# Expert choice of the first two batches inside the scan, and six of their eight tiles sent there by GpSimd

## What is computed

```python
def _L1_ffn_ref(hidden_states, gate_w, w_gate, w_up, w_down):    # E = 32, K = 8, 2048 rows
    probs = jax.nn.softmax(x @ gate_w, axis=-1)
    w, sel = jax.lax.top_k(probs, K)
    w = w / jnp.sum(w, axis=-1, keepdims=True)
    ...
    pos = jnp.arange(P) - start[se]          # rank of a row among those of its expert
    slot = jnp.where(pos < C, se * C + pos, E * C)
    ...
    g = jnp.einsum('ech,ehi->eci', xg, w_gate)
    u = jnp.einsum('ech,ehi->eci', xg, w_up)
    y = jnp.einsum('eci,eih->ech', jax.nn.silu(g) * u, w_down).reshape(E * C, H)
    out = jnp.zeros((T + 1, H), x.dtype).at[t_slot].add(w_slot[:, None] * y)
...
x = x + _L1_xattn_ref(ctx_1024, _layernorm(x, axis=-1), ...)     # the scan
x = x + _L1_ffn_ref(_layernorm(x, axis=-1), ...)                 # the experts
```

## Time and profile before

| | |
|---|---|
| median of 3 runs | 1883.29 us (1882.07 to 1884.48) |
| the profiled execution | 1881.68 us, span 1879.5 us |
| TensorE | 1554.0 us busy, 83% of the span |
| VectorE | 1308.7 us, 70% |
| ScalarE | 911.0 us, 48% |
| GpSimd | 791.8 us, 42% |
| sends of rows (L1474) | 128, 129.1 us busy, mean 1009 ns |
| mean granted clock of TensorE | 0.897 of full speed |

### The profile page before, as it was taken

The page is one execution under the profiler, slowest core; times in us unless marked ns, Lnnn a source line. Parts: engine busy times, 40 slices in busy tenths (PEclk is TensorE's granted clock), DMA queues, the critical chain, the costliest instruction groups (busy, mean ns, idle before and its releaser), DMA issues. The chain is left out here.

```text
span 1879.5 us, 26432 instructions
## 1 busy us (share of the span) xinstructions
PE 1554.0 (83%) x9418; PEld 1319.2 (70%) x9426; DVE 1308.7 (70%) x1901; ACT 911.0 (48%) x1577; POOL 791.8 (42%) x481
## 2 busy tenths in 40 slices
PE   5857778677528987996898799975899999999896
PEld 3444355454428976895897689855789999999785
DVE  6677586786659989999998999642445555555452
ACT  3444545445234444344444534432466666666463
POOL 1010000010045456445655643177735766762555
PEclk9878888888758997997999799987999999999998
DMA  7988799984682492375359236379998999999876
GB/s 213 343 281 275 274 321 368 333 270 157 210 314 95 175 357 74 119 283 222 106 188 370 82 118 218 145 266 338 382 365 232 250 269 253 256 260 223 226 170 85
DMA packets 187942, 445.48 MB, mean 237 GB/s; under 512 B 41616, under 2 KB 43664, under 8 KB 177568
## 3 DMA queue, kind: packets, MB, share of 16 engines
q1 hardware_dynamic: 115040, 283.37, 44.7%
q0 software_dynamic: 31760, 74.48, 16.8%
q10 hardware_dynamic: 41008, 85.89, 12.6%
HBM read 246.77 MB, written 205.28 MB: 241 GB/s over the span
## 5 line engine op out<-in xcount | busy, mean ns | idle before, releaser
L1441 POOL TENSOR_TENSOR mix_st<-mix_Bb,mix_du 128x2048 f32<-128x2048 f32 x64 | 293.3, 4583 | 268.2 <-DVE mix_st L2225 255.7
L2217 DVE TENSOR_TENSOR_SCAN mix_st<-mix_YY,mix_st 128x512 f32<-128x512 f32 x256 | 312.0, 1219 | 46.0 <-POOL mix_st L1441 24.0
L1895 ACT ACTIVATE mix_YY<-mix_dt,mix_A 128x512 f32<-128x512 f32 x256 | 176.9, 691 | 276.5 <-DVE mix_st L2217 272.3
L1492 POOL DMA_INDIRECT out_x<-moe_ys,moe_meta x130 | 210.5, 1619 | 190.1 <-ACT moe_ys L2032 84.6
L1611 PE MATMUL mix_G<-mix_xThi,mix_wup 128*128 128x256 f32 x1408 | 273.0, 291 | 14.5 <-issue 13.6
L1611 PEld LDWEIGHTS mix_G<-mix_xThi,mix_wup 128*128 128x128 f32 x1408 | 231.8, 199 | 17.6 <-issue 16.2
L1793 PE MATMUL mix_Dp<-moe_xhi,moe_whi 128*128 128x288 f32 x768 | 234.5, 305 | 2.0 <-ACT moe_xhi L1995 1.5
L1793 PE MATMUL mix_Dp<-moe_xhi,moe_wlo 128*128 128x288 f32 x768 | 228.9, 298 | 0.0
L1793 PE MATMUL mix_Dp<-moe_xlo,moe_whi 128*128 128x288 f32 x768 | 228.7, 298 | 0.0
L2357 DVE TENSOR_TENSOR moe_xlo<-mix_G,moe_xhi 128x512 fp32r<-128x512 f32 (+1 forms) x160 | 102.2, 638 | 170.5 <-ACT moe_xhi L1995 167.9
L1637 PE MATMUL mix_YY<-mix_ident,mix_st 128*128 128x128 f32 x1024 | 145.1, 296 | 86.2 <-DVE mix_st L2225 86.2
(11 more groups left out here) (237 smaller groups left out, 3064.9 us busy)
## 6 DMA issues: line engine op xcount, KB each, us to landing
x_by_expert<-front_zeros ACTq DMA_DIRECT2D x16, 4480.0 KB, 24.1
mix_wup<-w_halves SPq DMA_DIRECT2D x44, 1024.0 KB, 5.5
moe_raw<-in_ew SPq DMA_DIRECT2D x32, 1280.0 KB, 8.5
moe_xt<-x_by_expert SPq DMA_DIRECT2D x128, 256.0 KB, 8.6
mix_wdn<-w_halves SPq DMA_DIRECT2D x44, 512.0 KB, 6.4
front_idx<-in_idx SPq DMA_DIRECT2D x44, 384.0 KB, 9.0
w_halves<-front_wst SPq DMA_DIRECT2D x44, 384.0 KB, 7.9
mix_Bb<-bc_rows SPq DMA_DIRECT2D x16, 1024.0 KB, 9.4
```

The source lines that it names most:

```text
L1441: nc.gpsimd.tensor_tensor(st[:, g % STBUF, :, :], Bb[:, q, :, :], du[:, k % 2, :].unsqueeze(1).to_broadcast([P, NG, S]), ALU.mult).then_in ...
L1492: pool.indirect_dma_start(out=out_rows, out_offset=bass.IndirectOffsetOnAxis(ap=meta[0:rows, e % MBUF, j, 0:1].bitcast(U32), axis=0), in_= ...
L1895: nc.scalar.activation(dA, dt[:, k % 2, :], ACT.Exp, scale=A[:, c, m:m + 1]).then_inc(da_ready, 1)
L2217: nc.vector.tensor_tensor_scan(r, dA, r, 0.0, ALU.mult, ALU.add).then_inc(scanned, 1)
```

## The change

Batches 0 and 1 (`EARLY` = 2) are chosen in the slots of batches 2 and 3: their transposes at place 15 of the batch before and place 0, from `x2`; shift, exponent and the eight largest at place 1, ranks at place 2, places at place 3, weights at place 4. Their scratch lies in the half of `y` that is free then, and their logits and ranks in a bank of `T`, in which up products are formed from place 4 on. The stored rows get 560 columns; SP stores the columns of numbers and weights (`store_meta`) at place 5 and loads three tiles of a batch back (`load_waiting`) into a spent buffer, `xn` for tiles 0 to 2 and `y[:, 1]` for tiles 3 to 5. POOL sends from there in places 8 to 16, three sends in most slots (`SENDS_AT`), 24 per buffer. Tiles 6 and 7 (`ON_CHIP` = 2) are loaded into `XB` at the end of the scan and sent after it with batches 2 and 3, k outermost as before. POOL's constants are made at slot 6. The choice after the scan is that of batches 2 and 3 alone, with filler between them.

```diff
+EARLY = NB - 2
+STAGED = 3
+ON_CHIP = EARLY * TT - 2 * STAGED
+SENDS_AT = ({8: 3, 9: 2, 10: 3, 11: 3, 12: 3, 13: 3, 14: 3, 15: 3, 16: 1}, {9: 2, 10: 3, 11: 3, 12: 3, 13: 3, 14: 3, 15: 3, 16: 4})
...
+        waiting = [Place(nc, "mix_", at, at + 8192)(f"waiting{w}", [P, STAGED, PITCH], F32)
+                   for w, at in enumerate((row_at, small_at))]
...
-            bank = YY[:, b, :] if b < 2 else Dp[:, b - 2, :]
+            bank = T[:, 1, :] if b < EARLY else YY[:, b - EARLY, :]
...
+            def store_meta(b):
+                sp.wait_ge(meta_ready, b + 1)
+                sp.wait_ge(ids_made, 2 * b + 2)
+                sp.dma_start(s["XN"][b][:, D:PITCH].rearrange("(t p) n -> p t n", p=P), meta_of(b)).then_inc(meta_out, 16)
+
+            def load_waiting(w):
+                if w == 0:
+                    sp.wait_ge(zT_ready, TT * EARLY)
+                else:
+                    sp.wait_ge(x3_ready, NB - 1)
+                sp.wait_ge(xn_out, 16 * w + 16)
+                sp.wait_ge(meta_out, 16 * w + 16)
+                sp.dma_start(waiting[w][:, :, :], xn_rows[w * STAGED * P:(w + 1) * STAGED * P, :].rearrange(
+                    "(t p) n -> p t n", p=P)).then_inc(waiting_in, 16)
...
+                if l == 5 and b >= NB - EARLY:
+                    store_meta(b - 2)
+                if l == 7 + b - EARLY and b >= NB - EARLY:
+                    load_waiting(b - EARLY)
...
+            def early_ids(b):
+                pool.wait_ge(x3_ready, b + 1)
+                nc.gpsimd.iota(meta_of(b)[:, :, 0:1].bitcast(I32), pattern=[[P, TT], [1, 1]], base=b * S,
...
+            def send_waiting(w, first, end):
+                if first == 0:
+                    pool.wait_ge(filled, 16 * (FILLS + 2))
+                    pool.wait_ge(waiting_in, 16 * w + 16)
+                    pool.wait_ge(where_ready, w + 1)
+                for j in range(first, end):
+                    k, n = divmod(j, STAGED)
+                    send(w * STAGED + n, k, waiting[w][:, n, :])
+
+            def sends_on_chip(k):
+                if k == 0:
+                    pool.wait_ge(xb_in[0], 16)
+                for i in range(2 * STAGED, EARLY * TT):
+                    send(i, k, XB[:, i, :])
...
+                if l == 12 and 0 < b <= EARLY:
+                    early_ids(b - 1)
+                w, at = (b - EARLY, l) if l > 1 else (b - 1 - EARLY, l + UNITS)
+                if w >= 0 and at in SENDS_AT[w]:
+                    done = sum(n for slot, n in SENDS_AT[w].items() if slot < at)
+                    send_waiting(w, done, done + SENDS_AT[w][at])
...
+            done = sum(n for slot, n in SENDS_AT[1].items() if slot < UNITS)
+            send_waiting(1, done, STAGED * TOP)
             last_scale(2, 0)
+            sends_on_chip(0)
             last_scale(2, 1)
-            pool.wait_ge(ids_made, 2)
-            pool.wait_ge(filled, 16 * (FILLS + 2))
-            for k in range(TOP):
+            pool.wait_ge(ids_made, 2 * EARLY + 2)
+            sends(EARLY, 0)
+            sends(EARLY + 1, 0)
+            for k in range(1, TOP):
                 if k > 1:
                     pool.wait_ge(e_xT_ready, NT * (k - 2) + 2)
-                for b in range(NB):
-                    sends(b, k)
+                sends_on_chip(k)
+                sends(EARLY, k)
+                sends(EARLY + 1, k)
...
+                if h == 0 and b >= NB - EARLY:
+                    pe.wait_ge(rT_copied, TT * (b - 1))
+                if h == 1 and b >= NB - EARLY:
+                    pe.wait_ge(rank_read, b - 1)
...
+            def early_transposes(b, t):
+                n = TT * b + t
+                if t == 0:
+                    pe.wait_ge(norm_ready[2], TT * b + TT)
+                    pe.wait_ge(h_ready, HALVES * (b + 2) - 1)
+                else:
+                    pe.wait_ge(rT_copied, n)
+                for c in range(DC):
+                    last = nc.tensor.transpose(T[:, 0, c * P:(c + 1) * P], x2[:, t, c * P:(c + 1) * P], ident[:, :])
+                last.then_inc(rT_ready, 1)
...
+            def logits(b, t):
+                if b + t == 0:
+                    pe.wait_ge(g_in, 16)
+                if b < EARLY and t == 0:
+                    pe.wait_ge(h_ready, HALVES * (b + 2))
+                if b == EARLY and t == 0:
+                    pe.wait_ge(scanned, NG * ALL)
+                if b == EARLY + 1 and t == 0:
+                    pe.wait_ge(y_copied, NB * DC)
+                pe.wait_ge(rT_copied, TT * b + t + 1)
+                for c in range(DC):
+                    last = nc.tensor.matmul(choice_bank(b, 0, t, t + 1), columns(b, t)[:, c, :], gw[:, c, :],
+                                            start=(c == 0), stop=(c == DC - 1))
+                last.then_inc(logits_ready, 1)
+
...
+                if l == 0 and EARLY <= b < NB:
+                    early_transposes(b - 2, 2)
+                    logits(b - 2, 0)
+                    logits(b - 2, 1)
...
+                    if b >= EARLY:
+                        ranks(b - 2)
...
+                if l == UNITS - 1 and 0 < b <= EARLY:
+                    early_transposes(b - 1, 0)
+                if l == 0 and EARLY <= b < NB:
+                    early_transposes(b - 2, 3)
+                    logits(b - 2, 2)
...
+                if l == UNITS - 1 and 0 < b <= EARLY:
+                    early_transposes(b - 1, 1)
+                if l == 0 and EARLY <= b < NB:
+                    logits(b - 2, 3)
...
+            transposes_and_logits(EARLY)
             for t in range(TT):
                 last_z_transposes(t)
-            transposes_and_logits(1)
-            ranks(0)
-            transposes_and_logits(2)
-            transposes_and_logits(3)
+            ranks(EARLY)
+            pe.wait_ge(rT_copied, TT * (EARLY + 1))
+            stay_busy(20, T[:, 1, :])
+            transposes_and_logits(EARLY + 1)
-            for b in range(1, NB):
-                stay_busy(10)
-                ranks(b)
-            pe.wait_ge(rank_read, 1)
+            stay_busy(10, Dp[:, TT - 1, :])
+            ranks(EARLY + 1)
...
+                    if c == 0:
+                        act.wait_ge(logits_ready, TT * (b - 1))
+                    if c == 2:
+                        act.wait_ge(meta_out, 16 * (b - 1))
+                    if c == 3:
+                        act.wait_ge(where_ready, b - 1)
...
+                    if b == NB - 1 and t == 0:
+                        for k in range(TOP):
+                            act.wait_ge(sent[k], 16 * STAGED)
...
+                if b < EARLY and t > 1:
+                    act.wait_ge(logits_ready, n - 1)
+                stage = T[:, t % 2 if b >= EARLY else 0, :]
...
+                    if l == UNITS - 1 and 0 < b <= EARLY and t == 3:
+                        rows_to_columns(b - 1, 0)
+                    if l == 0 and b >= EARLY and t != 1:
+                        rows_to_columns(b - 2, max(1, t))
+                    if l == 1 and b >= EARLY and t == 1:
+                        exponent(b - 2)
...
+                        dve.wait_ge(rT_ready, TT * b)
...
+                if l == 1 and b >= EARLY:
+                    shift(b - 2)
...
+                if l == 1 and b >= EARLY:
+                    choose_top(b - 2)
+                if l == 3 and b >= EARLY:
+                    place_key(b - 2)
+                if l == 4 and b >= EARLY:
+                    row_weights(b - 2)
...
+                if l == 1 and b >= EARLY:
+                    choose_mask(b - 2)
+                if l == 3 and b >= EARLY:
+                    place_rows(b - 2)
...
+            shift(EARLY)
+            choose(EARLY)
+            row_weights(EARLY)
+            place(EARLY)
+            shift(EARLY + 1)
+            choose(EARLY + 1)
+            place(EARLY + 1)
+            row_weights(EARLY + 1)
```

276 lines of the change are left out of this document (144 added, 132 removed).

## The result

| | before | changed |
|---|---|---|
| median of 4 runs, us | 1882.88 | 1853.09 (1850.97 to 1854.28) |
| profiled execution, us | 1881.68 | 1852.71 |
| its span, us | 1879.5 | 1850.9 |
| first transposes of the first expert | 1242.09 | 1242.44 |
| first tile of the ninth expert | 1414.44 | 1383.48 |

The changed kernel takes 0.984 of the time before, interval 0.982 to 0.986: **29.8 us faster**. The median is 7 us above the forecast of 1846 and inside the range. (The prediction's "six experts later" is the ninth expert's first tile.

A forecast was written before the change was run, and what follows sets the result against it. PE and DVE bound the scan's second halves, PE the late experts; between them POOL's sends make PE wait. 1881.7 - 13.3 - 39.2 + 14.2 + 1.5 = 1844.9 us profiled, 1846 as a median, range 1830 to 1867.

The forecast's parts named there:

- The first expert earlier: After the scan: only batches 2 and 3 left to choose, fewer sends before the first expert; 13.3 us gained, bounds 9 to 15.
- Experts at PE's pace: Experts 1 to 6: 10 sends per round take 12.8 us, under PE's 17.59; 39.2 us gained in all.
- The 2 us of shorter waits and the 2.5 us of clock: First expert: shorter tile waits gain 2 us; less PE idling beforehand, so a faster clock, gains 2.5 (0 to 5).
- the allowance for DMA waits: Early experts: 4 us of waits left (bounds 0 and 12), as transfers need about 17.4 us of PE's 17.59.
- the DMA rival: Early experts: DMA sets their pace, periods 19.5 us instead of 17.59, 11.5 and 6 us lost, 1864; chance 0.13.
- The scan, +15.7: Batches 2 and 3 of the scan: costs of 14.2 us, plus 1.5 for waits and sends.
- (a): End of slot 15: ACT copies the first transposed tile before the next slot's first decay; 2.6 us a batch.
- (b): Slots 1, 3 and 4, where DVE is full: its choice, places, weights and shift cost 3.8 us a batch.
- (c): Slot 4: the new weight product stands ahead of DVE's product of states, beside POOL's work; 0.7 us a batch (0 to 1.7).
- The waits and sends: Scan: ACT's wait for all first sends 0.5 us (0 to 4), the sends themselves 1 us in all.
- POOL behind in the scan: Rival: sends over 1.51 us push POOL's product over DVE's; 7 slots per batch lose 1.8 us each, 1871; chance 0.12.
- The other rivals: Up weights starved (1898, chance 0.03), handshakes over 20 us a batch (0.02), early sends unfinished in the scan (1860, 0.04).

The follow-up runs named there:

- e10: Changed kernel with POOL's rounds of sends for experts 1, 2 and 3 cut in two by waits, at most five sends under way; 1871.83 us.
- e1: Changed kernel without PE's 20 filler products between batch 2's ranks and batch 3's transposes; last statistics to first transposes 28.58 us, 3.1 more than the changed kernel.
- e2: Changed kernel with the split of the first expert's weights moved earlier on ACT and DVE; end of logits to first transposes 16.29 us in place of 18.09.
- e4: Changed kernel with ACT's copy of the first transposed tile behind the next slot's first decay, not ahead; scan stretch 445.20 us in place of 448.22.
- e11: Changed kernel with the edits of e2 and e4 and a later gate for the send rounds of experts 3 to 7; 1852.45 us, 0.986 of the kernel before.
- e12: Changed kernel with the edits of e2 and e4 and the third expert's weights loaded behind its third tile; 1848.74 us, 0.983 of the kernel before.
- e6: Changed kernel without the 48 sends of tiles 0 to 5 in the scan; scan stretch 447.99 us, against 448.09 in e5.
- e9: The kernel before, unchanged, run again with its profile; scan stretch 436.08 us, against 436.07 in its first trace.
- e5: The changed kernel, unchanged, on a chip where the kernel before takes 1947.0 us; 1884.17 us, 0.968 of the kernel before.
- e3: Changed kernel with 68 filler products instead of 48 ahead of the first expert's tiles; first transposes 28.36 us after the statistics in place of 25.5.

## Why the prediction came out as it did

The gains were forecast 11.4 us too large and the costs in the scan 3.5 us too dear; these errors cancel in part, and the rest is the 7.8 us by which the profiled execution lies above 1844.9. The mechanisms were right in the main.

**What bounded the kernel.** Right. POOL's rounds of 16 sends were the pace of the first experts; with 10 a round the period is PE's 17.59 us from the fourth expert on. e10 shows the same from the other side: 25.1 us of waits put into three rounds make the stretch 18.4 us longer.

**The first expert earlier, -13.3: the mechanism right, the size 3.5 us too large.** Two steps were mis-sized, by 2.0 and 1.8 (the rest of the path came out 0.3 shorter). The logits of batch 3 end 7.4 us after the statistics (1216.95 to 1224.35), not 5.4: I had batch 3's transposes free at once, and PE was still at its middle filler, which is 1.4 of the 2.0. e1 shows that this is no plain loss, since without it the clock falls and the logits end 9.1 us after the statistics; leaving out that filler doesn't bring my 5.4. And the first send of batch 3 took 2.81 us where I had 1.27 with its gap: DVE's split of the first expert's weights, which I had put down as ending "at about 1221", started only at 1229.74, in the same microsecond. I had priced just this collision in the scan, from the earlier trace rows, and not here. e2 took it away and got back 1.80. The Trainium skill, SBUF — State Buffer, section "SBUF: two separate sides", has the lock held for the whole instruction; the trace agrees that the send waits to an instruction's end, 2.81 us against 0.97, and DVE's three operations of 0.98 weren't delayed. The trace goes further in one thing: the send doesn't get in between two operations that follow each other. In another it differs: the same section has it that DVE's `tensor_tensor` didn't stall a DMA, and here this very operation did; the measurement decides.

**Experts at PE's pace, -39.2: 7.9 us too large.** The wait of 13.28 us is gone in full. The 2 us of shorter waits and the 2.5 us of clock inside the first expert are almost not there: from the first transposes to the third expert's first tile it takes 27.49 us, against 28.11 before without that wait, 0.6 us of 4.5. The clock is still 0.53 there, and PE had idled for 4.14 us ahead of it, from the end of the filler at 1238.3, where I had "about a microsecond"; the long send is 1.8 of them. The other 4 us are the allowance for DMA waits, 4 of them forecast and 8.0 found (113.55 us for six periods of 17.59), 7.1 of them in the first period. That was inside my bounds of 0 and 12, but not my value. Only 4.8 of the 8.0 are waits for tiles (4.32 in the first period, 0.23 and 0.28 later). The other 2.8 of the first period hold no wait; they lie behind that of 4.32, where PE's granted clock is 0.57 (1276 to 1284). So this wait cost its own length and the slow microseconds after it, and my sum had no term for that. The reason that I had weighed, 17.4 us of transfers against 17.59, was right as a mean, and wrong for the first period: there the rounds of sends for two later experts, 1280 KB of weights and five tiles meet (share 1.02). So the DMA rival held in part, at the third expert only, and at 4.8 us of waits with 2.8 of clock behind them, of its 17.5.

**The scan, +15.7: 3.5 us too dear.** The slots of the last batch, from one of POOL's products of inputs to its next, in us:

| slot | 0 | 1 | 2 | 3 | 4 |
|---|---|---|---|---|---|
| before | 11.05 | 8.68 | 13.51 | 8.78 | 9.68 |
| changed | 13.45 | 10.18 | 13.21 | 9.81 | 10.94 |
| e4 | 11.97 | 10.17 | 13.22 | 9.82 | 10.92 |

(a) The late decay was seen where it was forecast, 2.62 us of DVE's idle time, and slot 0 is 2.4 us longer (2.3 in batch 2) where I had 2.6. The cause that I gave is 1.5 to 1.6 a batch of it (e4, e11 and e12), and 0.9 stays when the copy is moved. (b) and (c) were too dear: slots 1 to 4 are 3.5 us longer (3.6 in batch 2) where I had 4.5 (3.8 and 0.7); no run separates the two. That is 1.9 of the 3.5 us. The waits and sends, put at 1.5 us, cost 0.1 (e6), which is 1.4 more.

**POOL behind in the scan.** Its condition, a send over 1.51 us, was met: in slot 11 of the last batch a slot's three sends take 9.48 - 4.62 = 4.86 us, 1.62 each, the first of them 1.80 behind DVE's product. The collision that it feared came too, once a batch: in slot 10 DVE's product of states took 2.93 us, 1.7 more than in e6, because POOL's product was 2 us late (I had 1.2). So the price of 1.8 us was right for one slot and not for seven: in slots 11 and 12 DVE's product takes 1.55 us and then 1.20. And even in that slot it cost no time, since the scan is the same to 0.1 us without the sends. The step that failed is the way from a lag of DVE to the time, with the count of slots; the threshold and the collision were right. POOL's last product of the batch comes 1.1 us late, and the long slots at the end take that in.

**The other rivals.** Up weights landed in 7.0 us between 1120 and 1160, not 5.5, far from 12.8. The early sends ended in the scan as the diff says.

**What I can't account for.** -1.85 us ahead of the changed part and +2.36 behind the ninth expert. Both are what two executions differ by. The mark at 748.47 and 746.62 is at 746.62 in e9 too, which is the kernel before, and between 746.4 and 749.9 in all twelve runs. The last stretch was 465.06 and 464.8 in the kernel before, 466.0, 464.7 and 464.5 in e5, e11 and e12, and from 461.6 (e3) to 468.9 (e4) in the rest, e6 aside. Why two of the chips take 60 and 64 us longer for the kernel before, and one of them 31 for the changed one, isn't settled: e5 places it, in two parts, and the run that was to test the cause (e10) came to a chip that doesn't show it.

## What to carry to other kernels

When sends or loads are taken off a path, price the first period after it by what meets there, not by the mean: here the mean had slack, and the first period kept 7 of the 8 us lost, nearly 3 of them by the slower clock behind a wait. When you move a step, list what will run beside it at its new time; a collision that was priced in one place was missed in another, and cost 1.8 us. A collision of two engines has a price on the engine and another on the time: here 1.7 us of the one were 0 of the other. And before removing filler work that seems to be in the way, measure what the clock behind it is worth.

## What the runs showed of the hardware

- Two chips that run the same program were equal to 0.5 us in the scan and in the stretch behind it, and 23% apart in the expert stretch: 173.9 us and 141.0. On the slow kind ACT resumed 18.34 us after its table load (2.78 on the other), and PE stood still for 1 to 2.5 us between products with nothing named that it waited for, from 1256 to 1267; POOL's unbroken run of sends had ended at 1263.2. About half of the 31 us lies there, the other half in the periods from the fourth to the sixth expert's first tile on. On such a chip taking sends away from that stage is worth more: 0.968 of the time before, against 0.984.
- A POOL send that starts inside a DVE operation on two SBUF operands waits for it (1.80 us at 1146.76), and through the next one if that follows at once: 2.81 us for a send of 0.97, which ends 0.86 us after DVE's last. DVE's products with C that run under sends alone take 1.20 to 1.22 us, as they do in e6 without sends.
- A POOL product on two SBUF operands does hold DVE: DVE's product at 1135.27 ends 1.09 us after POOL's, which began first, and takes 2.93 us in place of 1.2. In the earlier trace rows POOL's two operations last 1.26 and 2.25 us: DVE's product waited for the first, and the second for DVE's product.
- In the stretch of batch 3's choice PE's clock was 0.50 without the filler ahead of it (e1) and 1.00 with it.
